# Three 3x3 convolutions composed into one 7x7 convolution, with the tap sums dealt out anew

## What is computed

```
x = x + mix(groupnorm(x))      # first layer
x = x + conv3x3(conv3x3(conv3x3(groupnorm(x), w1), w2), w3)   # second layer, zero padding of 1 at each
```

## Time and profile before

| | |
|---|---|
| median of 3 runs | 525.75 us (525.26 to 525.93) |
| span of the profiled execution, first to last instruction | 521.9 us |
| around the span (median less span) | 3.9 us |
| PE busy | 461.2 us, 88% |
| DVE busy | 396.1 us, 76% |
| ACT, POOL busy | 189.2 and 187.5 us, 36% each |
| mean granted TensorE clock | 0.972 of 2.4 GHz |

### The profile page before, as it was taken

The page is one execution under the profiler, slowest core; times in us unless marked ns, Lnnn a source line. Parts: engine busy times, 40 slices in busy tenths (PEclk is TensorE's granted clock), DMA queues, the critical chain, the costliest instruction groups (busy, mean ns, idle before and its releaser), DMA issues.

```text
span 521.9 us, 6931 instructions
## 1 busy us (share of the span) xinstructions
PE 461.2 (88%) x2543; PEld 338.6 (65%) x2543; DVE 396.1 (76%) x536; ACT 189.2 (36%) x337; POOL 187.5 (36%) x93
## 2 busy tenths in 40 slices
PE   1347594799999999999998999899999999999995
PEld 1247383757854887488756885689558846884871
DVE  2598988999999999888898999899898994121101
ACT  3522420474145415461427234731554132430210
POOL 2152807712692163218370447054641720000000
PEclk9999785799999999999999999999999999999999
DMA  5100002520008210541072102711271017108201
GB/s 156 41 2 4 0 1 80 117 55 22 20 6 195 52 40 2 130 112 52 5 173 67 48 5 52 167 28 41 52 160 42 1 37 171 40 1 187 58 3 41
DMA packets 38225, 32.22 MB, mean 62 GB/s; under 512 B 24112, under 2 KB 28720, under 8 KB 38192
## 3 DMA queue, kind: packets, MB, share of 16 engines
q1 hardware_dynamic: 38192, 31.77, 25.7%
HBM read 5.66 MB, written 4.19 MB: 19 GB/s over the span
## 4 chain that ended last, share of the span: by engine, by line
PE 70%; DVE 11%; issue 8%; POOL 4%; ACT 3%; SPq 2%; DMA 2%; DVEq 0%; POOLq 0%; ACTq 0%
PE conv_ps L415 35%; PE conv_ps L423 14%; PE agg_ps L489 9%; PE val_ps L474 5%; DVE prod L1093 5%; PE geo_ps L456 3%; PE pw_ps L504 2%; POOL prod L1998 2%; SPq L282 2%; PE conv_ps L437 1%; POOL xs L2014 1%; DMA xq<-y 1%; DVE prod L1103 1%; DVE y L1136 1%; DMA xraw<-in_x 1%
## 5 line engine op out<-in xcount | busy, mean ns | idle before, releaser
L1093 DVE TENSOR_TENSOR prod<-val_ps,tapw 128x2048 f32<-128x2048 f32 x80 | 180.5, 2283 | 5.9 <-PE val_ps L474 4.8
L1998 POOL TENSOR_TENSOR prod<-prod 128x2048 f32<-128x2048 f32 x23 | 105.3, 4579 | 128.8 <-DVE prod L1093 128.8
L415 PE MATMUL conv_ps<-c_hi,wc_hi 128*128 128x448 f32 (+1 forms) x240 | 91.8, 382 | 0.7 <-ACT c_lo L1726 0.7
L423 PE MATMUL conv_ps<-c,w_sb 128*64 128x512 f32 x384 | 89.7, 602 | 0.0
L2014 POOL TENSOR_TENSOR xs<-xn 128x1024 f32<-128x1024 f32 x32 | 71.0, 2226 | 52.1 <-DMA xn<-xn 21.3
L415 PE MATMUL conv_ps<-c_hi,wc_lo 128*128 128x448 f32 (+1 forms) x240 | 86.3, 359 | 0.0
L415 PE MATMUL conv_ps<-c_lo,wc_hi 128*128 128x448 f32 (+1 forms) x240 | 86.2, 359 | 0.0
L489 PEld LDWEIGHTS agg_ps<-ident_sb,prod 128*128 128x128 f32 x480 | 59.0, 151 | 23.0 <-issue 13.2
L489 PE MATMUL agg_ps<-ident_sb,prod 128*128 128x128 f32 x480 | 67.2, 290 | 6.0 <-DVE prod L1103 4.4
L415 PE MATMUL conv_ps<-xq,wc_hi 128*128 128x512 f32 x192 | 64.0, 414 | 5.1 <-DMA xq<-y 3.0
L1103 DVE TENSOR_TENSOR prod<-prod 128x2048 f32<-128x2048 f32 x27 | 61.6, 2286 | 0.4
(11 more groups left out here) (109 smaller groups left out, 456.7 us busy)
## 6 DMA issues: line engine op xcount, KB each, us to landing
xq<-y SPq DMA_DIRECT2D x128, 132.0 KB, 2.6
xraw<-in_x SPq DMA_DIRECT2D x32, 128.0 KB, 2.7
x2r<-x SPq DMA_DIRECT2D x128, 32.0 KB, 1.8
out_y<-x2r SPq DMA_DIRECT2D x32, 128.0 KB, 2.8
w_sb<-in_w SPq DMA_DIRECT2D x1, 576.0 KB, 5.0
xn<-xn SPq DMA_DIRECT2D x16, 24.8 KB, 1.8
prod<-in_w SPq DMA_DIRECT2D x1, 384.0 KB, 4.0
prod<-in_w SPq DMA_DIRECT2D x1, 192.0 KB, 2.5
```

The lines of the kernel that those rows point to most:

```text
L415: mm = nc.tensor.matmul(bank[:, 0:conv_cols(n)], weights, lo if part == 1 else hi, start=term == part == 0, stop=final and part == 2)
L423: mm = nc.tensor.matmul(bank[MID * rows:MID * rows + MID, :], w3_sb[:, at:at + MID], src, start=term == 0, stop=final)
L1093: v.tensor_tensor(dst, val.unsqueeze(2).to_broadcast([P, B, R, C]), wgt.unsqueeze(3).to_broadcast([P, B, R, C]), ALU.mult).then_inc(mult_d ...
L1998: p.tensor_tensor(product(i, TAPS * h + a), product(i, TAPS * h + a), product(i, TAPS * h + b), ALU.add).then_inc(add_g, 1)
```

## The change

It replaces the three convolutions by one 7x7 convolution in plain float32, and rewrites all five lists.

- *Weights.* w1, w2, w3 are composed on the chip at the start: `turn` (9 transposes), `first_weights(0..3)` (55 float32 matmuls of 32 or 96 columns: w2 with w3), `second_weights(n, part)` (13 blocks of 8 or 16 float32 matmuls of 32 to 160 columns: that with w1), taken out of PSUM by ScalarE (`take_turn`, `take_first`, `take_second`).
- *Convolution.* 60 terms an image, in two halves b of 32 columns of the image: 14 "main" terms (7 horizontal shifts times 2 blocks of rows), each a pair of 128x64 float32 matmuls of 512 columns; then 16 small terms that put the border right: 7 "rows" (32 columns), 6 "cols" (16 columns), 3 "corner" (1 column), pairs too. No splitting, no step between layers. The residual is folded in: the centre weights of an image get the standard deviation times the identity (`centre_weights`, VectorE), `result` on ScalarE adds the mean. `split_high`, `split_low`, `high_part`, `low_part`, `take_high`, `by_quads` go. The tile xq is doubled.
- *Tap sums.* From the third image on a half image's adds are GGGV and GGVG (six on GpSimd, two on VectorE) where they were GGVV and GVVT (three on GpSimd, four on VectorE, one on TensorE).

```diff
-SUMS = [("GTTT", "GTTT"), ("GGVT", "GVVT")] + [("GGVV", "GVVT")] * (IMAGES - 2)
+SUMS = [('GTTT', 'GTTT'), ('GGGT', 'GGVT'), ('GGGV', 'GGVG'), ...]
+DX_ORDER = (0, 1, 2, 4, 5, 6, 3)
+CONV = ([("main", t, dx) for dx in DX_ORDER for t in range(2)] + [("rows", 0, dx) for dx in range(MAIN)]
+        + [("cols", t, n) for n in range(3) for t in range(2)] + [("corner", 0, n) for n in range(3)])
...
+                for half in range(2):
+                    part = slice(2 * C * half, 2 * C * half + 2 * C)
...
+                    if kind == "main":
+                        cols = slice(m + b * W // 2, m + b * W // 2 + W // 2)
+                        w = wmid[:, j % 2, t, :] if m == MAIN // 2 else kb[:, t, LEFT + m, :]
+                        mm = nc.tensor.matmul(bank[part, :], w, src[:, every, cols], start=n == 0, stop=False)
+                    elif kind == "rows":
...
+                        mm = nc.tensor.matmul(bank[part, q * W // 2:(q + 1) * W // 2], kt[:, half, LEFT + m, :],
+                                              src[:, line, cols], start=False, stop=False)
```

The start of TensorE's list:

```diff
+            turn(0)
+            turn(1)
+            fold(0, 0)
             gn1_sums(0, 0)
+            first_weights(0)
             gn1_sums(0, 1)
+            first_weights(1)
             geometry(0)
             values(0, 0)
+            values(0, 1)
             gn1_sums(1, 0)
+            fold(0, 1)
+            first_weights(2)
             gn1_sums(1, 1)
-            fold(0, 0)
-            values(0, 1)
+            first_weights(3)
+            second_weights(0, 0)
```

and its end, where `convs(5, 56, 60)` stands ahead of `pointwise(7, 0)`:

```diff
+            pointwise(7, 0)
+            convs(6, 0, 10)
+            transpose_sums(7, 4)
+            transpose_sums(7, 5)
+            convs(6, 10, 11)
+            transpose_sums(7, 6)
+            transpose_sums(7, 7)
+            convs(6, 11, 13)
+            pointwise(7, 1)
+            convs(6, 13, 21)
...
+            convs(6, 28, 60)
+            convs(7, 0, 60)
```

More of the change, by code:

```diff
@@ L21 @@
 PW = W + 2
+PY = W + 6
 GEO = G * 4 * R
@@ L210, in left, with taken, placed, all_taken @@
             return [0] + [b for (a, b), who in zip(ADDS, SUMS[i][h]) if who == "T"]
[L212 to L241, removed]
+        def taken(n):
+            return sum(len(placed(i)) for i in ROWS2[n])
+        def placed(i):
+            if LEFT <= i < LEFT + MAIN:
+                return [(kb[C * s:C * s + C, t, :, C * r:C * r + C], s) for t in range(2) for r in range(2)
+                        for s in range(4) if 4 * t + s - r == i - LEFT]
+            side = 0 if i < LEFT else 1
+            r, s = EDGE[i][0], 1 + EDGE[i][1]
+            return [(kt[C * s:C * s + C, side, :, C * r:C * r + C], s)]
+        def all_taken(n):
+            return sum(taken(m) for m in range(n))
         block = ctx.enter_context(nc.Block())
@@ L361, in _ @@
             store(6)
-            by_quads(7)
             store(7)
[L364 to L370, removed]
-                rows, hi, lo, first = slice(1 + j0, 1 + j0 + m), xq_hi, xq_lo, 0
-            else:
-                rows, hi, lo, first = slice(j0 + t, j0 + t + m), c1_hi, c1_lo, 3
-            return first + term, hi[:, rows, cols], lo[:, rows, cols]
@@ L703, in _ @@
[L703 to L706 removed]
+            convs(1, 44, 51)
+            values(4, 0)
+            convs(1, 51, 52)
+            pointwise(3, 1)
+            convs(1, 52, 60)
+            values(4, 1)
+            gn2_sums(3, 0)
+            gn2_sums(3, 1)
+            gn1_sums(5, 0)
+            gn1_sums(5, 1)
+            convs(2, 0, 3)
+            geometry(5)
+            values(4, 2)
+            convs(2, 3, 6)
@@ L795, in _ @@
+            values(6, 1)
+            convs(3, 56, 60)
+            gn2_sums(5, 1)
+            convs(4, 0, 6)
+            gn1_sums(7, 0)
+            convs(4, 6, 8)
+            gn1_sums(7, 1)
+            convs(4, 8, 13)
             values(6, 2)
-            convs(4, 15, 18)
-            take_high(4, 3)
-            transpose_sums(5, 7)
+            convs(4, 13, 14)
+            geometry(7)
+            convs(4, 14, 15)
             values(6, 3)
-            convs(4, 18, 19)
-            pointwise(5, 1)
@@ L1570, in _ @@
             mult(7, 1)
+            residual(6, 1)
+            gn2_stats(6, 1)
+            gn2_spread(6)
             mult(7, 2)
-            residual(6, 0)
+            gn2_scale(6)
             mult(7, 3)
+            gn2_bias(6)
+            centre_weights(6)
             mult(7, 4)
```

1421 lines of the change are left out of this document (643 added, 778 removed).

## The result

The changed kernel takes 602.66 us (median of 4 runs, 600.72 to 604.83) against 525.5 us for the kernel before, run beside it: a ratio of 1.148 [1.144, 1.151], 77 us slower. I had forecast 553 us: the direction is right, the loss is nearly three times mine, and it lies outside my range.

What follows compares the result with a forecast made beforehand. TensorE bounds the old middle; afterwards VectorE and GpSimd shutting each other out would set 61 us an image. 45 + 101 + 5 x 61 + 47 + 45 + 6 = 549 us span, median 553; own range 535 to 582, overall 478 to 583.

Steps and rivals of the forecast that it cites:

- VectorE and GpSimd shut each other out: Middle images: VectorE instructions with two SBUF tensors and GpSimd tensor instructions cannot overlap; floor 50 us an image.
- A: Rival, middle images: the port costs only its floor, 50 us an image; whole 487 us; chance 0.17.
- B: Rival, whole kernel: no port effect to speak of, TensorE and VectorE balanced; 467 us; chance 0.10.
- two tensors from SBUF: The kind of VectorE instruction said to be shut out by GpSimd's tensor instructions, for the whole of the other's instruction.
- The walk of the lists: Middle images: VectorE's and GpSimd's lists followed in order, with waits, give 58 and 64, mean 61 us an image, against 55.1.
- The start: Up to the first mult: composing the weights delays geometry(0) to 27.5 us and the first mult to 45, not 31.9.
- Images 0 and 1: First two images, by the same walk: 44 and 57, together 101 us against 91.2.
- second_weights hides beside VectorE: Images 0 and 1: the 13 second_weights blocks cost nothing while TensorE waits; if not hidden, up to 13 x 1 us.
- The small pairs: Convolution: 32 small pairs an image at one geometry instruction's time each, 3.7 us an image.
- rival C: Convolution: small matmuls at geometry's price, 15.4 not 3.7 us an image; 559 us, or 577 with the walk; chance 0.09.
- The end: From image 7's first mult: 47 us to pointwise(7, 1), then 45 of TensorE's convolutions and 6 for last result and store.
- the four parts: Changes forecast by part: start +13, images 0 and 1 +10, five images +30, end -26 us.

Runs made afterwards that it cites:

- e1: Changed kernel with each of GpSimd's 43 adds of products on one column instead of 2048, sums left out: 513.8 us, ratio 0.980.
- e2: Changed kernel with each of GpSimd's adds replaced by two fills of the same 2048 columns, which read nothing: 519.9 us, ratio 0.993.
- e5: Changed kernel with the composition of the weights left out, one matmul kept of each first_weights and each half of second_weights' last parts: 584.6 us.
- after: The changed kernel itself, with no further edit: 602.7 us, ratio 1.148 to the kernel before.
- e6: Changed kernel with the same work reordered: gn1_sums(0) and geometry(0) ahead of the weights' turning, most of the composition and its ScalarE copies later: 597.1 us.
- e9: Changed kernel without the rows, cols and corner matmuls of the convolution (128 small instructions an image): 595.3 us.

## Why the prediction was right in direction and wrong in size

**VectorE and GpSimd shut each other out: right, and decisive.** e1 gives the adds 89 us, more than the whole loss, and e2 shows that it is not GpSimd's time as such. Rivals A and B fall. The Trainium skill (GPSIMD Engine Reference, Key points) names instructions in a 2-port mode or with two SBUF inputs. L993, with two, at 1.82 instead of 0.74 us, agrees. L957, a TENSOR_SCALAR with one SBUF input, takes 1.07 instead of 0.28 us; that it is in such a mode the profile doesn't say and no run shows, so the prediction's "two tensors from SBUF" was too narrow. B's price was wrong as well: e1 is nearest to its condition and takes 514 us, not 467. TensorE is busy there 235.1/5 = 47.0 us an image, not 44, and VectorE 44.6 + 5.3 of waits.

**The walk of the lists: its terms for an image were 42.2 of VectorE's own work, 19 of hold-ups and 0.5 of other waits.** Measured: the hold-ups are (69 + 25)/5 = 18.8, as walked; the own work is 295.6/5 - 18.8 = 40.3; the other waits are 32.1/5 = 6.4. The step that failed is the one that let VectorE wait for almost nobody but GpSimd: 30 us too little in five images. The own work, over-sized by 9, hid part of that by luck, and 3 went with rounding: the walk's first half adds up to 58.9, not 58, and the mean of the two to 61.7, not 61. The earlier trace rows had the number: 275.5 - 250.4, 5.0 us an image, in the kernel before; e1, without the adds' length, still has 5.3. The waits are uneven: 13.7 of the 32.1 us fall in image 5, which takes 74.1 us from mult to mult where the other four take 61.7 to 65.6. What makes them there is in the trace: in the stretch after 401 us TensorE stood 6.3 us for a copy of ScalarE's, which stood behind ScalarE's part of tap_weights, which waited 6.9 us for VectorE's parts, held by an add and pair sums; the residual then waited 4.2 us for TensorE:

```profile
401.33 3.56 DVE L957 TENSOR_SCALAR ch<-geo 128x128 f32<-128x128 f32 x1
405.00 2.21 DVE L962 TENSOR_SCALAR ch<-ch 128x128 f32<-128x128 f32 x1
407.13 2.10 DVE L965 TENSOR_TENSOR ch<-geo,small 128x128 f32<-128x128 f32 x1
409.15 2.09 DVE L969 SCALAR_TENSOR_TENSOR ch<-ch,geo 128x128 f32<-128x128 f32 x1
419.57 0.75 DVE L1084 SCALAR_TENSOR_TENSOR x<-pw_ps,pw_b_sb,xraw 128x512 f32<-128x512 f32 x1 [4.20 <-PE pw_ps L513]
...
413.48 1.97 PE L498 MATMUL agg_ps<-ident_sb,prod 128*128 128x128 f32 x8 [6.34 <-ACT agg L1649]
415.38 3.12 PE L428 MATMUL conv_ps<-xq,wmid 128*64 128x512 f32 x8
...
409.26 0.31 ACT L1591 ACTIVATE ch<-ch 128x128 f32<-128x128 f32 x1 [6.87 <-DVE ch L965]
412.85 1.06 ACT L1649 ACTIVATE agg<-agg_ps 128x512 f32<-128x512 f32 x2
```

Behind that idle the eight main instructions took 3.12 us, not the 1.9 to 2.0 of other such eights: the granted clock is 1.00 from 400 to 407 us, 0.51 from 410.9 to 417.8 and 1.00 again behind it. Over the five images it is 0.87 of full (2.4 GHz), in e1 0.97, and the same instructions keep TensorE busy 263.6 us, not 235.1. How much of the waits is this lower clock's no run separates.

**The start: 59.0, not 45.** Two steps failed. first_weights(1), which I had at 0.13 us an instruction, takes 10.87/50 = 0.22, and geometry(0) 3.67, not 2: geometry(0) ends at 33.7 instead of 27.5. These were prices of TensorE's higher clock, taken too early: even geometry(1) takes 3.68 us, at 51.1 here and at 35.6 in the kernel before. And tap_weights(0) takes 25 us instead of the 17.5 left: I had counted pair sums against it, not what stands in other queues.

```profile
19.23 10.87 PE L375 MATMUL conv_ps<-w_sb 64*128 64x96 f32 x50
30.03 3.67 PE L463 MATMUL geo_ps<-geo_w_sb,xc 128*128 128x64 f32 x16
36.03 6.61 PE L375 MATMUL conv_ps<-w_sb 64*128 64x96 f32 x30
42.57 0.58 PE L529 MATMUL geo_ps<-gn,sel_sb 128*128 128x1 f32 x2
...
43.19 0.16 DVE L900 TENSOR_SCALAR gn<-geo_ps 128x1 f32<-128x1 f32 x1 [4.56 <-PE geo_ps L529]
48.53 0.29 DVE L996 TENSOR_TENSOR trig<-trig 128x128 f32<-128x128 f32 x1 [4.29 <-ACT trig L1607]
```

gn1_scale(1) stands in VectorE's list between parts 11 and 12 of tap_weights(0) and waited for gn1_sums(1, 1) behind first_weights(2); ScalarE's part 4 stood behind its copies of first_weights(2) and (3). e5 bears it out in part: the first mult comes 27.1 us later than in the kernel before; without the composition it comes 12.2 us earlier than in after, and in the order of e6 17.3.

**Images 0 and 1: 108.6, not 101.** Image 0 is 43.8, as forecast. Image 1 took 64.9, not 57: VectorE 55.0 busy and 9.9 waiting; in e1 58.2, so 6.7 go with the adds. That second_weights hides beside VectorE was nearly right in this order (in e5 62.4 for image 1, 45.3 for image 0: 1 us less for both) and stopped being so when it was moved (e6).

**The small pairs: right.** 0.114 us against 0.115; rival C falls (e9).

**The end: 49.2 + 56.0, not 47 + 51.** 1.0 us of the 5 behind pointwise(7, 1) is a wait for ScalarE's copy out of the bank, and the run of 48 main instructions behind it took 12.35 us, its like 10.7.

The errors of the four parts, 14, 8, 23 and 7 us, point one way, so they didn't cancel; my range was built from each term's own bounds.

## What to carry to other kernels

A GpSimd instruction that reads two SBUF tensors costs VectorE not its length but what VectorE has to do meanwhile: nothing beside mults out of PSUM, nearly all of it beside a chain of short SBUF instructions. So ask of each add which product it needs and what VectorE's list holds at that moment, before counting busy shares. And when walking one engine's list, add the waits that it already has in the kernel before, and write down for each wait what else stands in the queue of the engine waited for.

## What the runs showed of the hardware

A fill of GpSimd (1.81 us for 2048 columns) and an add hold up different instructions of VectorE. In e2 nine TENSOR_SCALAR instructions of 128x128 from SBUF to SBUF (L958, L963, L976) started inside a fill more than 0.3 us before its end, and each ended 0.08 us behind it. Instructions on two SBUF tensors were not held: four V adds that started inside a fill kept their 2.28 us, and seven L896 their 0.22, where an add holds L895 up to 4.45 us. The mults out of PSUM were held by neither: 25 started inside an add in after, none over 2.29 us. That it is the reading that makes the difference for two tensors follows from add against fill; why a TENSOR_SCALAR of 128x128 is held by both, and one of a single column (L905, 0.12 and 0.21 us inside a fill) is not, no run shows.

From 0 to about 90 us the page gives TensorE a granted clock of nearly full, and yet geometry(0) takes 3.67 us, twice the 1.93 of the earlier trace rows, and the four transposes of a `values` take 1.06 to 1.11 us until 69 us and 0.66 at 71; they take 1.11 at 90.3, where the clock is given as 0.50. So in an early stretch its own rows (0.22 us an instruction) are a better price than the clock that the page shows.
